# A one-core decoder layer: the RMS factors and gates are turned on VectorE by 32 by 32 blocks instead of through TensorE and DRAM, and some orders are rewritten

## The reference, cut to what matters

```
h = x * rsqrt(mean(x*x) + 1e-6) * norm_w                 # "rms": one factor per token
q, k, v = heads(h Wq), heads(h Wk), heads(h Wv)           # 8 heads of 64; q and k get a rope
beta, ig, og = sigmoid(h Wbeta + b), sigmoid(h Wig + b), sigmoid(h Wog + b)   # 8 gates each, per token
M_t = M_{t-1} * beta_t + ig_t * scale * k_t v_t ;  y_t = (q_t M_t) * og_t
x = layernorm(x + y Wout + bout)
x = layernorm(x + x * running_sum(0.9, ctx * ctx))
x = layernorm(x + gelu(xn W1 + b1) W2 + b2)               # 8 experts, 512 tokens each
```

## Time and profile before

| what | value |
|---|---|
| median of 3 runs | 1244.49 us |
| the profiled execution: its own time | 1243.14 us |
| its span (first to last instruction) | 1241.3 us, mean granted TensorE clock 0.997 |
| busy: PE, DVE, ACT, POOL | 98%, 63%, 37%, 61% of the span |
| expert stage, 550 to 1225 us | PE busy 25.00 of 25 us in every stretch of 25 us |
| attention stage, 150 to 475 us | PE busy 24.5 to 25.0 of 25 us, DVE 21.6 to 24.0 |
| 500 to 525 us | PE busy 19.18 of 25 us, granted clock 0.86 |

### The profile page before, as it was taken

The page is one execution under the profiler, slowest core; times in us unless marked ns, Lnnn a source line. Parts: engine busy times, 40 slices in busy tenths (PEclk is TensorE's granted clock), DMA queues, the critical chain, the costliest instruction groups (busy, mean ns, idle before and its releaser), DMA issues.

```text
span 1241.3 us, 18919 instructions
## 1 busy us (share of the span) xinstructions
PE 1212.5 (98%) x6682; PEld 1017.4 (82%) x6682; DVE 784.5 (63%) x1201; ACT 455.7 (37%) x597; POOL 756.0 (61%) x519
## 2 busy tenths in 40 slices
PE   8989999999999999899999999999999999999998
PEld 7778888888888888678888888888888888888886
DVE  5889898888888888753544544634734536445424
ACT  5233333323332332444434443534435344344320
POOL 4887777777777775458447265284385384482651
PEclk9999999999999999899999999999999999999999
DMA  8778787777777776237316326245064073163310
GB/s 277 161 156 175 164 171 149 165 153 169 153 164 164 162 161 180 79 129 257 102 56 231 95 104 204 75 161 190 31 238 142 0 279 101 46 238 97 115 55 34
DMA packets 178106, 179.51 MB, mean 145 GB/s; under 512 B 44732, under 2 KB 121484, under 8 KB 178060
## 3 DMA queue, kind: packets, MB, share of 16 engines
q1 hardware_dynamic: 177548, 178.64, 52.7%
q10 hardware_dynamic: 512, 0.26, 0.1%
HBM read 137.55 MB, written 17.18 MB: 125 GB/s over the span
## 4 chain that ended last, share of the span: by engine, by line
PE 83%; DVE 5%; issue 2%; POOL 1%; ACT 0%; DVEq 0%; POOLq 0%; ACTq 0%
PE score_ps L88 18%; PE score_ps L89 18%; PE score_ps L90 18%; PE qk_ps L88 7%; PE qk_ps L89 7%; PE qk_ps L90 7%; PE score_ps L1526 3%; PE score_ps L1575 2%; DVE decays L1172 1%; PE score_ps L1579 1%; DVE rot L1143 1%; DVE rot L1142 1%; DVE probs L1172 0%; PE score_ps L1458 0%; PE score_ps L1460 0%
## 5 line engine op out<-in xcount | busy, mean ns | idle before, releaser
L1380 DVE CAST hid_hi<-score_ps 128x512 fp32r<-128x512 f32 x124 | 85.6, 690 | 335.1 <-ACT score_ps L824 335.1
L824 ACT ACTIVATE score_ps<-score_ps,b_cols 128x512 f32<-128x512 f32 x128 | 84.5, 660 | 362.2 <-PE score_ps L90 361.3
L1032 POOL TENSOR_TENSOR w_lo<-w_raw,w_hi 128x2048 fp32r<-128x2048 f32 x31 | 143.2, 4620 | 97.8 <-ACT w_hi L784 97.8
L88 PE MATMUL score_ps<-xnT_hi,w_hi 128*128 128x512 f32 x512 | 199.6, 390 | 1.0 <-issue 1.0
L89 PE MATMUL score_ps<-xnT_lo,w_hi 128*128 128x512 f32 x512 | 199.2, 389 | 0.0
L90 PE MATMUL score_ps<-xnT_hi,w_lo 128*128 128x512 f32 x512 | 199.2, 389 | 0.0
L1116 DVE TENSOR_TENSOR_SCAN decays<-f_all,diag 128x384 f32<-128x384 f32 x128 | 161.2, 1290 | 0.6
L88 PE MATMUL qk_ps<-xT_parts,wqkv_hi 128*128 128x256 f32 x512 | 148.9, 291 | 11.0 <-DVE rot L1143 7.6
L1024 POOL TENSOR_TENSOR w_lo<-w_raw,w_hi 128x2048 fp32r<-128x2048 f32 x32 | 147.7, 4616 | 12.3 <-ACT w_hi L794 12.3
L89 PE MATMUL qk_ps<-xT_parts,wqkv_hi 128*128 128x256 f32 x512 | 144.7, 283 | 0.0
L90 PE MATMUL qk_ps<-xT_parts,wqkv_lo 128*128 128x256 f32 x512 | 144.5, 282 | 0.0
(11 more groups left out here) (186 smaller groups left out, 2680.6 us busy)
## 6 DMA issues: line engine op xcount, KB each, us to landing
w_raw<-in_w SPq DMA_DIRECT2D x64, 1024.0 KB, 7.7
f_all<-f_dram SPq DMA_DIRECT2D x16, 1024.0 KB, 4.8
qkT<-rot SPq DMA_DIRECT2D x256, 64.0 KB, 2.5
xT_raw<-in_xT SPq DMA_DIRECT2D x16, 512.0 KB, 12.0
x_both<-in_x SPq DMA_DIRECT2D x16, 512.0 KB, 10.9
f_all<-f_dram SPq DMA_DIRECT2D x16, 512.0 KB, 6.0
c_both<-in_ctx_in SPq DMA_DIRECT2D x16, 512.0 KB, 12.5
x_both<-x_dram SPq DMA_DIRECT2D x8, 1024.0 KB, 4.9
```

What stands on the lines that cost most here:

```text
L88: eng.matmul(out, lhs_hi, rhs_hi, start=first, stop=False)
L824: act.activation(up_ps[c % 2][:], up_ps[c % 2][:], ACT.Gelu, bias=b1_cols[:, bass.ds(e.after(FC, c), 1)]).then_inc(gelu_done, 1)
L1032: pool.tensor_tensor(w1_lo[s % 2][:], w1_raw[s % 2][:], w1_hi[s % 2][:].bitcast(F32), ALU.subtract)\
L1380: dve.tensor_copy(high, up_ps[c % 2][:]).then_inc(hid_hi_done, 1)
```

## The change

`rms_on_rows`, `turn_gates` on TensorE, `store_rms`, `spread_rms` and `load_g` go, with their DRAM tensor and semaphores. VectorE gets two new functions of four transposes each, 32 partitions at a time (64 columns): `turn_rms` reads the rms columns, broadcast along 32 columns, from partitions 0, 32, 64 and 96 and writes rows at partition 0; `turn_gates` reads the gate rows at partition 0 and writes tokens at partitions 0, 32, 64 and 96. `gates` and `rms_rows` grow to 32 partitions. `turn_rms(b + 1)` stands right before `sum_gates(b + 1)` in every body, `turn_gates(b)` before rope 0 in bodies 2 to 15.

Beside that, orders change: rope 1 goes between the two weightings; in body 1 the gates of sequence 2 are summed three scans earlier and ScalarE computes them before `grow_memory(0)`, GpSimd and SyncE work in another order; in body 15 ScalarE normalizes the expert's tokens after the second `y_high`, VectorE takes the token statistics before rope 3 and puts scans behind `y_low`; in body 16 `scale_x2` goes behind the second `gelu`; on TensorE `turn_tokens` goes ahead of `cross_memory`.

```
-            def load_g(b):
-                for j in range(NT):
-                    sp.dma_start(g_raw[:, j, :], rows[j * P:(j + 1) * P, :], allow_slow_non_contiguous=True).then_inc(g_in, 16)
...
                 if b.n == 1:
-                    store_rms(b + 1)
                     load_ctx(b)
                     move(b, 0)
-                    spread_rms(b + 1)
+                    move(b, 1)
                     load_xT(b + 2)
+                    move(b, 2)
+                    move(b, 3)
+                    spread_f(b + 1)
                     load_x(b + 2)
-                    move(b, 2)
-                    move(b, 1)
-                    move(b, 3)
+                    store_o(b + 1)
+                    spread_o(b + 1)
...
-                    if (b - 2).within(B) and b.n <= B and c == (2 if b.n == B else 0):
+                    if (b - 2).within(B) and b.n <= B - 1 and c == 0:
                         scale_x2(b - 2)
-                    if b.n == B - 1 and c == 2:
+                    if b.n == B - 1 and c == 3:
                         expert_normalize(Step(0), 0)
                     if b.n == B and c in (1, 3):
                         gelu(Step(0), c // 2)
+                    if b.n == B and c == 3:
+                        scale_x2(b - 2)
...
+                if (b + 1).within(B):
+                    gate(b + 1)
                 if b.n == 1:
                     grow_memory(b - 1)
-                if (b + 1).within(B):
-                    gate(b + 1)
...
-                elif b.n >= 1 and r == (2 if b.n == 1 and b.i is None else 1):
+                elif b.n >= 1 and r == 1:
                     pool.wait_ge(s_mm, (b - 1).after(KC, KC))
...
                 if b.n == 1:
                     x_low(b + 1)
-                    residual(b)
+                    context_low(b - 1)
...
+            def turn_rms(b):
+                dve.wait_ge(rms_done, b.after(1, 1))
+                if b.n >= 1:
+                    dve.wait_ge(orow_done, (b - 1).after(1, 1))
+                rows = rms_rows[:].rearrange("r (j a t) -> r a j t", j=NT, t=SQUARE)
+                for a in range(GROUPS):
+                    column = rms[a * SQUARE:(a + 1) * SQUARE, b.odd, :].unsqueeze(2)
+                    last = dve.transpose(rows[:, a], column.broadcast_to([SQUARE, NT, SQUARE]))
+                last.then_inc(rms_turned, 1)
+
+            def turn_gates(b):
+                dve.wait_ge(gates_done, b.after(1, 1))
+                rows = gates[:].rearrange("g (j a t) -> g a j t", j=NT, t=SQUARE)
+                for a in range(GROUPS):
+                    last = dve.transpose(g_turned[a * SQUARE:(a + 1) * SQUARE], rows[:, a])
+                last.then_inc(gates_turned, 1)
...
@@ second
-                scans(b, 4, 5, 6, 7)
+                scans(b, 4)
+                turn_rms(b + 1)
                 sum_gates(b + 1)
+                scans(b, 5, 6, 7)
...
@@ middle
+                turn_gates(b)
                 rope_parts(b, 0)
                 weigh_half(b - 1, 0)
+                rope_parts(b, 1)
                 weigh_half(b - 1, 1)
-                rope_parts(b, 1)
                 clear_f(b)
                 scans(b, 0, 1)
                 rope_parts(b, 2)
-                scans(b, 2, 3)
-                rope_parts(b, 3)
                 if last:
                     token_stats()
                     token_means()
+                else:
+                    scans(b, 2, 3)
+                rope_parts(b, 3)
                 y_low(b - 1, 0)
-                scans(b, 4)
+                scans(b, 2 if last else 4)
                 y_low(b - 1, 1)
                 token_gates(b)
                 gate_v(b, 0)
                 if last:
+                    scans(b, 3, 4)
                     gate_v(b, 1)
...
                     gate_v(b, 1)
+                    turn_rms(b + 1)
                     sum_gates(b + 1)
...
-                if b.n == 1:
-                    rms_on_rows(b)
-                elif b.n >= 2:
-                    mm.then_inc(gates_ps, 1)
...
                 if (b - 1).within(B):
                     project_out(b - 1)
-                if b.n in (1, B - 1):
-                    cross_memory(b - 1)
                 if b.n == B - 1:
                     turn_tokens(Step(0), 2)
                     turn_tokens(Step(0), 3)
+                if b.n in (1, B - 1):
+                    cross_memory(b - 1)
```

More of the change, by code:

```diff
@@ L173, in layer_program @@
     wg_raw = sb("wg_raw", [P, KC, NG])
+    g_turned = over("g_turned", [P, NT, SQUARE], F32, home["wg_raw"])
     normw = sb("normw", [P, KC])
@@ L684, in gate @@
                         act.wait_ge(decay_done, (b - 1).after(NH, NH))
-                    if b.n <= 2:
-                        act.wait_ge(gates_turned, (b - 1).after(1, 1))
+                    act.wait_ge(gates_turned, (b - 1).after(1, 1))
                     act.wait_ge(orow_done, (b - 1).after(1, 1))
-                act.activation(gates[:], gates_sum[:], ACT.Sigmoid, bias=gate_bias[:]).then_inc(gates_done, 1)
+                if b.n == 0:
+                    act.wait_ge(gates_zero, 1)
+                act.activation(gates[0:NG, :], gates_sum[:], ACT.Sigmoid, bias=gate_bias[:]).then_inc(gates_done, 1)
                 act.wait_ge(gates_done, b.after(1, 1))
@@ L1076, in sum_gates @@
                 dve.wait_ge(gates_added, b.after(1, 1))
[L1077 to L1081 removed]
+                dve.wait_ge(rms_turned, b.after(1, 1))
+                dve.tensor_tensor(gates_sum[:], gates_sum[:], rms_rows[0:NG, :], ALU.mult).then_inc(gates_summed, 1)
@@ L1083, in token_gates @@
+            def turn_gates(b):
[4 more added lines that the diff above has]
+                last.then_inc(gates_turned, 1)
             def token_gates(b):
[L1084 to L1087 removed]
+                dve.wait_ge(gates_turned, b.after(1, 1))
@@ L1461, in gate_products @@
                                    start=False, stop=k == KC - 1)
-                if b.n == 1:
-                    rms_on_rows(b)
-                elif b.n >= 2:
-                    mm.then_inc(gates_ps, 1)
-            def rms_on_rows(b):
-                pe.wait_ge(rms_done, b.after(1, 1))
-                for j in range(NT):
-                    mm = pe.matmul(gate_ps[0:NG, L + j * P:L + (j + 1) * P], rms[:, b.odd, j:j + 1].broadcast_to([P, NG]),
-                                   ident[:], start=True, stop=True)
-                mm.then_inc(gates_ps, 1)
-            def turn_gates(b):
-                pe.wait_ge(gates_done, b.after(1, 1))
-                if b.n <= 1:
-                    pe.wait_ge(orow_done, b.after(1, 1))
-                for j in range(NT):
-                    mm = pe.matmul(gate_ps[:, L + j * NG:L + (j + 1) * NG], gates[:, j * P:(j + 1) * P],
-                                   ident[0:NG, 0:NG], start=True, stop=True)
-                mm.then_inc(gates_turned, 1)
+                mm.then_inc(gates_ps, 1)
             def project_share(b, g):
-                if b.n == 0 and g == 2 * KC:
-                    rms_on_rows(b)
-                if b.n == 0 and g == 4 * KC:
-                    turn_gates(b)
                 (n, j), part = (FIRST_SHARES if b.n <= 1 else SHARES)[g // KC], g % KC
@@ L1605, in slot @@
                     project_share(b, 3 * n + 2)
-                    if n == 2 and b.n == 1:
-                        turn_gates(b)
                 if b.n == 1 and n == 1:
```

63 lines of the change are left out of this document (18 added, 45 removed).

## The result

The changed kernel takes 1253.78 us in the median of 4 runs (1250.38 to 1255.10), the kernel before 1244.79 on the same chip: a ratio of 1.0068, 95% interval [1.0048, 1.0088]. It is slower by about 9 us; 5 us faster was forecast. The profiled execution of the changed kernel is the shortest of the four, 1250.38 with a span of 1248.6.

The account below looks back on a forecast made before the run. TensorE was taken as the bound, busy 1212.5 of 1241.3 us, so only idle and low-clock time could move. End -8.8, loop +0.2 and start +3.6 gave -5.0: 1239.5 us from 1244.49, range 1232.5 to 1245.

Parts of the forecast that it names:

- the start: Bodies before body 3: later VectorE groups and gates ahead of grow_memory(0) delay body 2's first share; net +3.6 us.
- The start's own mechanism: Body 2's first share starts 6.3 us later, after some 5 idle; 1.6 remains, plus 2 for a low clock.
- The end: Bodies 15 and 16: TensorE waits and a low clock worth 9.9 us go, 1.1 comes back; net -8.8.
- The 0.95 at the expert's first product: Body 16: TensorE's 0.95 us wait goes because the tokens are turned ahead of cross_memory.
- The new wait for v: Body 15: gate_v(15, 1) stands behind scans 3 and 4, so turn_tokens waits for it, 1.1 us.
- The loop: Twelve loop bodies: 4.7 us of rope waits go, 4.9 us of excess from turns comes; net +0.2.
- rope 1's place: Loop: rope 1 ahead of half 1 of the weighing removes the rope waits, 4.7 us in twelve bodies.
- the turns: Loop: two groups delay the next k share by 0.81 us in every other body, 4.9 in twelve.
- has no cover: Loop: turn_rms, right ahead of the sums, adds its full 0.9 us to the chain ending a body.
- is mostly hidden: Loop: rope 3's 0.74 us wait for the GpSimd covers turn_gates (0.9), so only 0.16 comes through.
- The price of a turn: VectorE: a group of four 64-column transposes takes 0.9 us, 0.21 each without overlap.
- D: Rival: turns are dear, 0.40 us a transpose and 1.6 a group, giving a slower 1249.8 us; chance 0.09.

Follow-up runs that it names:

- e2: Changed kernel with one input of the gate sums, and the turned gates of sequences 0 and 1, in PSUM: 1246.04 us, ratio 1.0021 to the kernel before.
- e5: Changed kernel with SyncE's load of x for sequence 3 issued ahead of the moves of q: 1248.01 us, ratio 1.0035 to the kernel before.
- e3: Changed kernel with ScalarE's old order in body 1, grow_memory of sequence 0 ahead of the gates of sequence 2: 1253.31 us, ratio 1.0080.
- e4: Changed kernel with consumers' inputs in PSUM and grow_memory of sequence 0 ahead of the gates of sequence 2: 1245.66 us, ratio 1.0017.
- e11: Changed kernel with consumers' inputs in PSUM (P) and the early load of x (Q), ScalarE's changed order kept: 1241.70 us, ratio 0.9979.
- e6: Changed kernel with consumers' inputs in PSUM, the early load of x and grow_memory of sequence 0 ahead of sequence 2's gates: 1241.96 us, ratio 0.9979.
- e7: Kernel before with only the changed order of bodies 15 and 16, no turns on VectorE: 1235.90 us, ratio 0.9945.
- e8: Kernel before with the changed order of bodies 15 and 16 and rope 1 between the weightings, no turns on VectorE: 1231.45 us, ratio 0.9903.
- e10: Changed kernel with the loop's rms turn behind the gates' turn instead of right ahead of the sums: 1255.74 us, ratio 1.0094.
- e12: Kernel before with changed end and rope 1 between the weightings, plus body 15's second gate_v ahead of scans 3 and 4: 1233.54 us, ratio 0.9920.
- e9: Changed kernel with all four transposes of the rms turn reading partitions 0 to 31, other tokens' factors left out: one run, 1247.53 us, not compared.

## Why the prediction was wrong

**The step that failed** is the start, as the prediction put it: "With two groups more it is done at 72.5; the gates, then `grow_memory` 1.02 later ..., then 0.83: the share starts at 74.4, 6.3 later". The term was +3.6, and 13.9 was measured. VectorE's last scan of body 1 ended at 76.02 + 2.64 = 78.66, and the share came at 80.93. The two groups were counted right. What was not counted is what the change does to their consumers. It takes the input of three of them from PSUM to SBUF, and brings the fourth, which had its inputs there, beside a GpSimd operation; VectorE waits for the GpSimd, 8.46 us at four places. e2 removes these waits, 3.1 us of them only by passing them on. The prediction priced the sums at 0.41 out of the earlier trace rows, a row at which the GpSimd happened to be idle; the scans' mean of 1.29 against the 0.94 or so of one alone was the hint that neighbours on the GpSimd count.

**The second hole** is a queue that the prediction did not follow: the new order in SyncE's list put x of sequence 3 behind the gates of sequence 2. The prediction has no term for it. It cost 2.35 at body 3's share in the trace and more in the runs (e5).

**The start's own mechanism**, that `grow_memory(0)` behind the gates makes TensorE wait 5 us, is in the trace (5.81, and 0.50 behind it), but e3, e4 and e11 show that its price was 0: VectorE's way through body 2 was late anyway. The prediction had said that VectorE's own path through bodies 1 and 2 "gives 2.7 to 3.6 as well"; it then is the only price. With P and Q taken out (e11), body 2's share comes at 74.61 behind a wait of 5.42, as forecast (74.4, some 5), and body 3's is 4.3 late where +3.6 was put: near, but not by the step that was priced, since without that wait (e6) it is 4.0.

**The end** held: -8.8 worked out, -9.0 in the traces, -8.1 in e7, by the steps named but one. No `yT_lo` wait is left and the clock stays at 1.00 there. The 0.95 at the expert's first product did not go: 1.12 now comes ahead of the scores in front of it (the L1502 "issue" above) and 0.27 at the product. The new wait for v is 0.41 (0.78 in e7, 1.88 in e8) where 1.1 was put.

**The loop** stayed inside its range (+0.2 forecast, -4.7 to +5 stated, +2.3 measured), with both terms too small: rope 1's place gives 6.5 in the traces (4.5 in the medians of e7 and e8) instead of 4.7, and the turns cost 8.8 instead of 4.9. That the sum is so near is in part luck, since the two errors pull against each other. The waits for `c_both` do come by turns, first nothing and 1.28 or 1.00, from 276 on about 0.36 and 0.70, rather than nothing and 0.81. That `turn_rms` "has no cover" and `turn_gates` "is mostly hidden" was the wrong picture: by e10 it makes no difference which of the two places a turn has. The gap in front of rope 3 (0.73 in a body of e8) is gone in the changed kernel, and the two turns of 1.92 together cost 0.73.

**The price of a turn** was right: 0.9 forecast, 0.95 to 0.97 measured. The slower rival, D, asked for dear turns; slower it became by another way, one that no rival had.

## What to carry to other kernels

When work is moved between engines, look at where its consumers' inputs lie afterwards, not only at its own price: an operand that goes from PSUM to SBUF can make a 0.41 us operation on VectorE wait out a 2.4 or 4.6 us one of the GpSimd, and leaving the intermediate sum in PSUM gave 6 us of the time back in this kernel. Look at the next operation with two inputs in SBUF as well: a part of the wait passed on to it. A wait of TensorE, even the longest, is worth something only if the engine that it waits for is not late at the next meeting point as well: undo it alone before you believe its length. A load behind a step that waits for late data becomes late itself, so every reordered DMA queue wants a line in the sum.

## What was not expected of the hardware

VectorE's small operations ended 0.03 to 0.29 us after a GpSimd operation that had begun before them, at four places where all their inputs lay in SBUF, and at none of the four with one input in PSUM (e2), although the same GpSimd operation still ran; the scan behind took 1.00 and 1.74 of it over. An idle TensorE of the same length was followed by a granted clock of 1.00 in one run (2.17, e8) and of 0.55 in another (2.16, e12). Transposes of 32 by 64 follow each other at 0.14 us on the same partitions and at 0.24 us when each starts on another group of 32 (e9).
